# Cross attention over 32 batches: half-tile score banks, a third maximum bank, a new order of projections, and the maximum split on the vector engine

## The reference, cut to what matters

```python
x = _layernorm(x + self_attention(x))            # one head, causal mask
x = _layernorm(x + cross_attention(x, ctx_1024)) # 16 heads of 8, relative bias
x = _layernorm(x + ffn(x))                       # 128 -> 512 -> 512 -> 512 -> 128, gated

# cross attention, for each of the 32 batches
q = shape(query_states @ wq, T); k = shape(key_value_states @ wk, S); v = shape(key_value_states @ wv, S)
scores = jnp.einsum('bhtd,bhsd->bhts', q, k) + bias        # T = 56, S = 1500
weights = jax.nn.softmax(scores, axis=-1)
attn = jnp.einsum('bhts,bhsd->bhtd', weights, v)
return attn.transpose(...).reshape(B, T, D) @ wo
```

## Time and profile before

| | |
|---|---|
| median of 3 runs | 1085.17 us (1084.59 to 1091.04) |
| the profiled execution | 1093.1 us, its span 1091.3 us |
| PE busy | 969.3 us, 89% of the span |
| DVE busy | 721.8 us, 66% |
| ACT busy | 605.5 us, 55% |
| POOL busy | 421.6 us, 39% |
| mean granted TensorE clock | 0.952 of 2.4 GHz |

### The profile page before, as it was taken

The page is one execution under the profiler, slowest core; times in us unless marked ns, Lnnn a source line. Parts: engine busy times, 40 slices in busy tenths (PEclk is TensorE's granted clock), DMA queues, the critical chain, the costliest instruction groups (busy, mean ns, idle before and its releaser), DMA issues. The chain is left out here.

```text
span 1091.3 us, 25611 instructions
## 1 busy us (share of the span) xinstructions
PE 969.3 (89%) x10410; PEld 657.2 (60%) x10410; DVE 721.8 (66%) x1510; ACT 605.5 (55%) x1071; POOL 421.6 (39%) x418
## 2 busy tenths in 40 slices
PE   6754579999999999999999999989999988799996
PEld 3542256666666666666666666666666666545564
DVE  6565447878778877878778878876777774540014
ACT  2321157666667666666666666666666656352232
POOL 7330535554444555554444555554444400000000
PEclk9866689999999999999999999998999999899999
DMA  7507665555666655555665755554665420300000
GB/s 228 192 10 163 117 190 178 164 177 178 191 177 204 185 176 179 163 178 178 191 194 161 209 179 177 164 179 147 188 181 162 137 78 2 109 1 1 1 9 25
DMA packets 57388, 156.10 MB, mean 143 GB/s; under 512 B 23936, under 2 KB 36152, under 8 KB 54200
## 3 DMA queue, kind: packets, MB, share of 16 engines
q1 hardware_dynamic: 56744, 152.85, 48.1%
q10 hardware_dynamic: 528, 1.63, 0.4%
HBM read 111.63 MB, written 42.63 MB: 141 GB/s over the span
## 5 line engine op out<-in xcount | busy, mean ns | idle before, releaser
L769 ACT ACTIVATE e_sb<-st_ps 128x896 f32<-128x896 f32 (+1 forms) x384 | 354.1, 925 | 153.0 <-DVE st_ps L714 93.5
L108 DVE TENSOR_REDUCE cmax<-max_ps 112x1 f32<-112x512 f32 x512 | 337.6, 683 | 150.5 <-PE max_ps L98 150.4
L98 PE MATMUL max_ps<-kst,qst 111*112 111x512 bf16 x760 | 283.8, 401 | 37.8 <-PEq L117 14.1
L611 PEld LDWEIGHTS st_ps<-qst,kst 114*128 114x128 bf16 (+1 forms) x3072 | 191.7, 101 | 88.7 <-issue 41.8
L821 POOL TENSOR_TENSOR kpart<-k_left,kpart 128x500 bf16<-128x500 f32 x90 | 102.7, 1141 | 352.4 <-ACT k_left L787 347.8
L611 PE MATMUL st_ps<-qst,kst 114*128 114x112 bf16 (+1 forms) x3072 | 215.7, 213 | 19.5 <-DMA qst<-nmp 18.3
L105 DVE CUSTOM_DVE_ANT_0 near_out<-max_ps,near_nat 112x476 bf16<-112x476 f32 x248 | 154.0, 649 | 26.4 <-PE max_ps L98 26.4
L98 PEld LDWEIGHTS max_ps<-kst,qst 111*112 111x112 bf16 x760 | 92.2, 130 | 106.8 <-DVE cmax L108 38.9
L641 PE MATMUL pv_ps<-e_sb,vals 128*32 128x168 f32 (+1 forms) x3072 | 150.0, 313 | 0.3 <-ACT e_sb L769 0.3
L685 PEld LDWEIGHTS misc<-wv,ctxt 128*128 128x128 f32 (+1 forms) x768 | 99.6, 193 | 15.8 <-ACT vals L754 11.8
L641 PEld LDWEIGHTS pv_ps<-e_sb,vals 128*32 128x32 f32 (+1 forms) x3072 | 80.4, 109 | 47.1 <-issue 34.6
(11 more groups left out here) (127 smaller groups left out, 941.1 us busy)
## 6 DMA issues: line engine op xcount, KB each, us to landing
kst<-kparts SPq DMA_DIRECT2D x192, 375.0 KB, 6.2
kparts<-kpart SPq DMA_DIRECT2D x90, 375.0 KB, 2.7
ctxt<-in_ctxT SPq DMA_DIRECT2D x32, 750.0 KB, 7.4
qst<-qslots SPq DMA_DIRECT2D x192, 28.0 KB, 6.4
qslots<-qst SPq DMA_DIRECT2D x4, 672.0 KB, 11.2
kparts<-kst SPq DMA_DIRECT2D x6, 375.0 KB, 3.1
h<-in_h SPq DMA_DIRECT2D x2, 1024.0 KB, 8.6
qst<-nmp SPq DMA_DIRECT2D x96, 1.8 KB
```

Of the source, the lines that this page charges most:

```text
L98: return nc.tensor.matmul(dst[0:TT, 0:hi - lo], m.qst[0:M_ROW, r, p, :], m.kst[0:M_ROW, r, p, lo:hi], start=True, stop=True)
L108: return nc.vector.tensor_reduce(m.cmax[:, r, c, p:p + 1], src[0:TT, 0:BOUND[c + 1] - BOUND[c]], AX.X, ALU.max)
L611: mm = nc.tensor.matmul(st_ps[0:K, j % 2, p // 4, (p % 4) * TT:(p % 4 + 1) * TT], m.kst[0:AUG, u % RING, p, j * P:j * P + K], m.qst[0:AUG, ...
L769: nc.scalar.activation(e_sb[0:K, j % E_RING, :].rearrange("p (a c) -> p a c", a=2), st_ps[0:K, j % 2, :, 0:HALF], ACT.Exp).then_inc(s_ex, 1)
```

## The change

- `st_ps` becomes three single banks. A tile's scores are made in two halves of 4 pairs, half h of tile j being number w = 2 x (12 b + j) + h, in bank w mod 3; each half is signalled, waited for and exponentiated by itself (448 columns). PE waits before a half until exponential w - 3 is done. The near additions are made by halves too.
- `max_ps` and `near_out` have three buffers; a chunk waits for the reduction three before it.
- `misc` in the steps 0 to 6: v, k, v, k, v, k, den (was v, v, v, den, k, k, k). In the iteration ahead of batch 0 the keys are at steps 1, 3, 5. The reciprocals are made in steps 6 and 7 (were 4 and 5), x_own and its sums in step 10 (was 9).
- The negated maximum is split into three bfloat16 parts by DVE before it is transposed, by four operations on 112 x 8, each waiting for the one before. PE transposes the 24 columns with a bfloat16 identity, ACT makes one copy (two before), and one DMA (three before) brings the three rows to `qst`. POOL's split of the maximum is gone, and POOL makes all three key splits before the multiplication by `own`.
- On ACT the copy of `pv_ps` in step 1 comes after the copies for `misc`.

The core of the diff:

```diff
 E_RING = 4
...
         PAIRED = ST // 2
-        HEAD_MISC = {4: ("k", 0, 3), 5: ("k", 1, 3), 6: ("k", 2, 3), M0: ("nmt", 0, 1),
+        HEAD_MISC = {1: ("k", 0, 3), 3: ("k", 1, 3), 5: ("k", 2, 3), M0: ("nmt", 0, 1),
                      9: ("v", 0, 1), 10: ("v", 1, 1), 11: ("v", 2, 1)}
-        MISC = {0: ("v", 0, 1), 1: ("v", 1, 1), 2: ("v", 2, 1), 3: ("den", 0, -1),
-                4: ("k", 0, 3), 5: ("k", 1, 3), 6: ("k", 2, 3), M0: ("nmt", 0, 1)}
-        NM, REC_A, REC_B, XH = M0 - 1, 4, 5, 9
+        MISC = {0: ("v", 0, 1), 1: ("k", 0, 3), 2: ("v", 1, 1), 3: ("k", 1, 3), 4: ("v", 2, 1), 5: ("k", 2, 3),
+                6: ("den", 0, -1), M0: ("nmt", 0, 1)}
+        NM, REC_A, REC_B, XH = M0 - 1, 6, 7, 10
...
                 if j == 0:
-                    pe.wait_ge(s_md[u % 2], filled(g, u, 2, 48))
-                wait(pe, s_ex, batch(g, u) * ST + j - 1)
+                    pe.wait_ge(s_md[u % 2], filled(g, u, 2, 16))
                 K = st_rows(j)
-                for p in range(PAIRS):
-                    mm = nc.tensor.matmul(st_ps[0:K, j % 2, p // 4, (p % 4) * TT:(p % 4 + 1) * TT],
-                                          m.kst[0:AUG, u % RING, p, j * P:j * P + K],
-                                          m.qst[0:AUG, u % RING, p, :],
-                                          start=True, stop=True)
-                mm.then_inc(s_st, 1)
+                for h in range(2):
+                    w = 2 * (batch(g, u) * ST + j) + h
+                    wait(pe, s_ex, w - ST_BANKS + 1)
+                    for p in range(4):
+                        mm = nc.tensor.matmul(st_ps[0:K, w % ST_BANKS, p * TT:(p + 1) * TT],
+                                              m.kst[0:AUG, u % RING, 4 * h + p, j * P:j * P + K],
+                                              m.qst[0:AUG, u % RING, 4 * h + p, :],
+                                              start=True, stop=True)
+                    mm.then_inc(s_st, 1)
 
             def max_chunk(g, u, item):
 
...
+                wait(pe, s_mr, batch(g, u + lag) * CHUNKS + n - MAX_BANKS + 1)
+                max_scores(nc, m, max_ps[:, n % MAX_BANKS, :], r, c, p).then_inc(s_mx, 1)
 
             def value_pair(g, u, t):
 
                 n = batch(g, u)
-                wait(pe, s_ex, n * ST + t + 2)
+                wait(pe, s_ex, 2 * (n * ST + t + 2))
                 if t == 0:
                     wait(pe, s_xr, n)
                     wait(pe, s_ve, 3 * n + 3)
...
                         pe.wait_ge(s_nm, n + 1)
-                        nc.tensor.transpose(misc[0:PAIRS, 0:TT], nmax[:, :], m.ident[0:TT, 0:TT]).then_inc(s_nt, 1)
+                        pe.wait_ge(s_ib, 1)
+                        nc.tensor.matmul(misc[0:3 * PAIRS, 0:TT], nm3[:, :, :].rearrange("q i p -> q (i p)"),
+                                         ident_b[:, :], start=True, stop=True).then_inc(s_nt, 1)
 
...
-                        dve.wait_ge(s_st, b * ST + j + 1)
-                        if j == 0:
-                            t, near = st_ps[:, 0, :, 0:HALF], m.near_t0[:, :].rearrange("p (a c) -> p a c", a=2)
-                        else:
-                            t = st_ps[0:NEAR - P, 1, :, 0:HALF].rearrange("p a (h t) -> p a h t", t=T)
-                            t = t[:, :, :, T - NEAR + P:T]
-                            near = m.near_t1[:, :].rearrange("p (a h t) -> p a h t", a=2, t=T)
-                            near = near[:, :, :, T - NEAR + P:T]
-                        nc.vector.tensor_tensor(t, t, near, ALU.add).then_inc(s_nb, 1)
+                        for h in range(2):
+                            w = 2 * (b * ST + j) + h
+                            dve.wait_ge(s_st, w + 1)
+                            if j == 0:
+                                t, near = st_ps[:, w % ST_BANKS, 0:HALF], m.near_t0[:, h * HALF:(h + 1) * HALF]
+                            else:
+                                t = st_ps[0:NEAR - P, w % ST_BANKS, 0:HALF].rearrange("p (h t) -> p h t", t=T)
+                                t = t[:, :, T - NEAR + P:T]
+                                near = m.near_t1[:, h * HALF:(h + 1) * HALF].rearrange("p (h t) -> p h t", t=T)
+                                near = near[:, :, T - NEAR + P:T]
+                            nc.vector.tensor_tensor(t, t, near, ALU.add).then_inc(s_nb, 1)
                     if j == XH and live(g, u - 1):
                         dve.wait_ge(s_ro, b)
                         nc.vector.tensor_tensor(x_own[:, :], x_sb[:, :], rec[:, :], ALU.mult).then_inc(s_xo, 1)
                     for lag, n, c, p in max_items(g, u, j):
                         dve.wait_ge(s_mx, (b + lag) * CHUNKS + n + 1)
-                        reduce_scores(nc, m, max_ps[:, n % 2, :], (u + lag) % 2, c, p).then_inc(s_mr, 1)
+                        reduce_scores(nc, m, max_ps[:, n % MAX_BANKS, :], (u + lag) % 2, c, p).then_inc(s_mr, 1)
                     if j == NM and live(g, u + 1):
                         dve.wait_ge(s_mr, (b + 2) * CHUNKS)
                         wait(dve, s_nt, b + 1)
+                        wait(dve, s_nm, b + 1)
                         nc.vector.tensor_reduce(nmax[:, :], m.cmax[:, (u + 1) % 2, :, :].rearrange("q c p -> q p c"),
-                                                AX.X, ALU.max, negate=True).then_inc(s_nm, 1)
+                                                AX.X, ALU.max, negate=True).then_inc(s_n0, 1)
+                        dve.wait_ge(s_n0, b + 2)
+                        nc.vector.tensor_copy(nm3[:, 0, :], nmax[:, :]).then_inc(s_n1, 1)
+                        dve.wait_ge(s_n1, 2 * b + 3)
+                        nc.vector.tensor_tensor(nm_left[:, :], nmax[:, :], nm3[:, 0, :], ALU.subtract).then_inc(s_n1, 1)
+                        dve.wait_ge(s_n1, 2 * b + 4)
+                        nc.vector.tensor_copy(nm3[:, 1, :], nm_left[:, :]).then_inc(s_n2, 1)
+                        dve.wait_ge(s_n2, b + 2)
+                        nc.vector.tensor_tensor(nm3[:, 2, :], nm_left[:, :], nm3[:, 1, :], ALU.subtract).then_inc(s_nm, 1)
                     if live(g, u - 1):
                         if j == REC_A:
                             dve.wait_ge(s_dr, b)
...
                     if live(g, u):
-                        w = b * ST + j
-                        if j < 2:
-                            act.wait_ge(s_nb, 2 * b + j + 1)
-                        act.wait_ge(s_st, w + 1)
+                        K = st_rows(j)
                         wait(act, s_pv, b * PAIRED + j // 2 - 1)
-                        K = st_rows(j)
-                        nc.scalar.activation(e_sb[0:K, j % E_RING, :].rearrange("p (a c) -> p a c", a=2),
-                                             st_ps[0:K, j % 2, :, 0:HALF], ACT.Exp).then_inc(s_ex, 1)
-                    if j == 1 and live(g, u - 1):
-                        act.wait_ge(s_pv, b * PAIRED)
-                        wait(act, s_xo, b - 1)
-                        nc.scalar.copy(x_sb[:, :], pv_ps[:, 0:PIECES * T]).then_inc(s_xr, 1)
+                        for h in range(2):
+                            w = 2 * (b * ST + j) + h
+                            if j < 2:
+                                act.wait_ge(s_nb, 4 * b + 2 * j + h + 1)
+                            act.wait_ge(s_st, w + 1)
+                            nc.scalar.activation(e_sb[0:K, j % E_RING, h * HALF:(h + 1) * HALF],
+                                                 st_ps[0:K, w % ST_BANKS, 0:HALF], ACT.Exp).then_inc(s_ex, 1)
                     user = misc_user(g, u, j)
...
                             if live(g, u):
-                                act.wait_ge(s_md[u % 2], filled(g, u, 2, 48))
-                            nc.scalar.copy(nmp[:, 0, :], misc[0:PAIRS, 0:TT])
-                            nc.scalar.copy(nm_left[:, :], misc[0:PAIRS, 0:TT]).then_inc(s_nr, 1)
+                                act.wait_ge(s_md[u % 2], filled(g, u, 2, 16))
+                            nc.scalar.copy(nmp[:, :], misc[0:3 * PAIRS, 0:TT]).then_inc(s_nr, 1)
+                    if j == 1 and live(g, u - 1):
+                        act.wait_ge(s_pv, b * PAIRED)
+                        wait(act, s_xo, b - 1)
+                        nc.scalar.copy(x_sb[:, :], pv_ps[:, 0:PIECES * T]).then_inc(s_xr, 1)
 
             run(iteration)(act)
...
+            nc.gpsimd.tensor_copy(ident_b[:, :], m.ident[0:TT, 0:TT]).then_inc(s_ib, 1)
...
                 b = batch(g, u)
                 split_k(g, u, 0)
+                split_k(g, u, 1)
...
                     pool.wait_ge(s_ro, b)
-                split_k(g, u, 1)
-                if live(g, u + 1):
-                    done = 3 * (b + 1)
-                    pool.wait_ge(s_nr, b + 2)
-                    nc.gpsimd.tensor_tensor(nmp[:, 1, :], nm_left[:, :], nmp[:, 0, :],
-                                            ALU.subtract).then_inc(s_np, 1)
-                    pool.wait_ge(s_np, done + 1)
```

(14 more changed lines are left out.)

20 lines of the change are left out of this document (10 added, 10 removed).

## The result

The changed kernel takes 1122.91 us, median of four runs (1121.5 to 1125.14); the kernel before took 1087.73 on the same chips. The ratio is 1.0325, 95% interval 1.0281 to 1.0369: 3.3% slower. The profiled execution took 1121.78 us with a span of 1120.0.

The account below looks back on a forecast made before the run. PE with its waits was taken as the bound; the changed loop, 14.71 + 11.03 = 25.75 us against 24.5, gave +1.25 a batch, +35 over 28 batches, less about 4: 1085.2 + 31 = 1116 us, range 1078 to 1140.

Parts of the forecast that it names:

- The loop: Second half of S1 to den's copy on PE and ACT, then DVE back to S1: 25.75 us a batch against 24.5.
- first part: PE and ACT from the second half of S1 (second tile's scores) to the end of den's copy: 14.71 us.
- one ahead of nmt: PE's wait before the maximum's transpose, for DVE's split: 1.23 us, or 1.5 with DVE's lateness by the reciprocal.
- The key wait: PE after each key projection, waiting for ACT's copies: 0.48 us each, three replacing one, +0.96 us of PE per batch.
- the chain: Four dependent DVE operations on 8 columns that split the maximum: 4 x 0.20 = 0.80 us.
- the 4 us that the forecast took off for the end: 1.9 us for a wait at 912.23 and about 2 for the batches without key projections.
- This decides: Reciprocals (1.11 and 0.84 us) and maximum split on DVE now stand just ahead of the dense steps 8 to 11.
- PE with these pieces is the bound: Kernel before: 21.9 us of PE work a period plus some 2.6 us of standing still in pieces.
- nobody waits for that room: POOL's key splits start earlier, giving POOL and SP's stores of key parts room that was said to be unneeded.
- 1 (DVE never behind): Rival, chance 0.17: only misc order and maximum split cost, 24.6 us a period, about 1084 us, up to 1096.
- 2 (little comes back): Rival, chance 0.15: waits go, nmt's wait is 0.43 to 0.91, period 23.8 to 24.3 us, 1061 to 1075 us.
- 3: Rival, chance 0.10: waits cost more than their length, by score-half hand-overs or a lower granted clock, 1130 to 1152 us.

Follow-up runs that it names:

- after_nmt9: The changed kernel with nmt at step 9 instead of step 8: 1120.9 us, ratio 1.0288.
- best_4_2: `old_direct` with the third key projection at step 7, nmt at step 9, four half-tile score banks and two maximum banks: 1069.73 us, ratio 0.9832.
- no_recip: The changed kernel with both reciprocals cut to one column: 1110.58 us, ratio 1.0207.
- banks_alone: The kernel before with only the three half-tile score banks and three maximum banks: 1084.08 us, ratio 0.9962.
- old_direct: The kernel before with the change's banks, one DMA for the maximum rows and a one-part bfloat16 maximum written by the reduction: 1051.23 us, ratio 0.9645.
- no_split: `old_order` with POOL's three operations per key part cut from 500 columns to one: 1073.41 us, ratio 0.9869.
- one_part_direct: The changed kernel, new order kept, with a one-part bfloat16 maximum written by the reduction instead of the four-operation split: 1093.56 us, ratio 1.0036.
- old_order: The changed kernel with the old order of projections and reciprocals, and the old order on ACT and POOL: 1171.19 us, ratio 1.0772.

## Why the prediction was right, and where it was not

Forecast was a regular period of 25.75 us, from a loop; measured 25.74. Forecast were 1116 us, measured 1122.91.

*The loop, right in its course; that it fits to 0.01 is luck.* The forecast's first part runs from the second half of S1 (535.89) to the end of den's copy (550.53 + 0.39): 15.03 us, 14.71 forecast. From there to the next second half (561.63) are 10.71, 11.03 forecast. Each part missed by 0.32, and the two misses cancel. The waits were where they were said to be: three behind the keys, one ahead of nmt (1.39 in the prediction's way of counting, forecast 1.23, or 1.5 with DVE's lateness), one for a maximum bank in step 0 (0.18, forecast 0.5), one of 0.23 by its row and 0.39 from start to start at the second half of S1. An exponential of 448 columns takes 0.554, and the near additions 1.16 for two. `after_nmt9` supports the loop: it took away the largest of PE's waits and the period did not move.

*The key wait, mis-sized by 0.10.* From a key projection to the next S are 0.84 and then 2.30 (538.42 to 540.72) with 0.83 + 0.89 of work in them, so a wait costs 0.58, not 0.48: a projection that starts behind one takes 0.10 longer. The earlier trace rows show that already, 0.94 from 553.50 to the next S against 0.84 from 551.35. Two of these waits lie in the first part of the sum (0.20), and the copies and exponentials behind the third key add 0.08. What made up for them lies on DVE: the chain's links are 0.205 apart as forecast, but the second reciprocal starts 0.70 after the first of them and not 0.80 (554.24, inside the last one), and from it to the near addition are 6.08 and not 6.24. (The prediction's own parts of its 1.31, 0.20 + 0.47 + 0.58, are 1.25.)

*The 7 us between 1116 and 1123.* A fourth run of the kernel before took 1090.29 and moved its median from 1085.17 to 1087.73: 2.6 of the 7. The rest is the difference of the medians, 35.2 where 31 was forecast. The two traces divide theirs (28.7) by the near additions. The 28 periods from the second batch on add 26.1: 28 x 1.23 = 34.4, less 8.3 us by which some batches of the kernel before are longer than 24.51. The first period adds 2.4 and the last two take off 4.1. The stretch behind the last near addition adds 3.9, the one ahead of the first 0.4. So the 4 us that the forecast took off for the end were right, and it left out the first batch and the end of the block. Of the 3.9, 2.8 lie behind the last copy of `pv_ps`, where no edit was made; in the thirteen traces this last stretch takes between 162.2 and 168.3 us. (The forecast's average of 24.72 took the last start of the earlier trace rows, 913.8, for that of an addition like the first; it is the small one of tile 1.)

*The longer batches, not explained in the forecast.* The 8.3 us are six of the 28 periods of the kernel before, 24.73 to 27.16 long. The longest, 27.16, ends with this wait (timeline of the kernel before):

```profile
737.45 0.93 PE L611 MATMUL st_ps<-qst,kst 114*128 114x112 bf16 x8 [2.52 <-DMA qst<-nmp]
```

The maximum rows came late, PE stood still, and the granted clock from 737.40 to 741.00 was 0.50. At 815.06 PE waited 1.64 for them. The two kernels with three DMAs for the rows wait for them in nearly every batch; the eleven with one DMA show a single such wait behind the first batch (0.67, at the end of `best_4_2`), and the changed kernel's 31 periods are 27 of 25.74 and four shorter ones. The forecast put this transfer at 0.24 to 0.5 a batch and 1.9 once. Whether the median run of the kernel before has fewer long batches no trace shows.

*"This decides", wrong.* The reciprocals at steps 6 and 7 lay in the loop, as worked out, and yet they decided next to nothing (`no_recip`, 0.25 us). A second loop, without them, was only 0.25 shorter. The sum was right because the longer one was found; the reason given for it was not the one that a remedy could have used.

*What bounds the kernel before, incomplete.* "PE with these pieces is the bound" overlooked that the maximum rows' way through POOL and three DMAs was as long. The wait of 0.24 at 563.33 was counted as a small piece that goes away. It was the visible end of a loop that takes back most of a gain elsewhere: the banks bring 0.27 with it (`banks_alone`) and 24.35 - 23.33 = 1.02 without it.

*The balance, by runs.* From 24.51: banks and direct rows -1.18 (`old_direct`), the chain +0.82 (`no_split`, `one_part_direct`), the new order +1.59 (`one_part_direct` against `old_direct`). Together 24.51 - 1.18 + 0.82 + 1.59 = 25.74; these are steps from run to run, so they must add up, and only the chain's term was measured twice. Of the order's 1.59, two more key waits at 0.58 are 1.16 if they add, and the second halves of S1 and the reciprocals are candidates for the rest, which no run divides.

*What the prediction did not see at all* is what the new order is good for. It said of POOL's earlier splits that nobody waits for that room. With the split on DVE, it is all-important: at the old places the chain meets POOL's key splits and costs 3.98 (27.31 - 23.33), at the new places POOL is done just in time (its last split of the period runs from 552.20 to 553.33, the first cast starts at 553.54) and it costs 0.82. So the order costs 1.59 us where the chain is absent and gains 1.57 where it is present.

*The rivals.* 1 (DVE never behind) fell with DVE's timeline. 2 (little comes back) fell at the chain, 0.82 where it needed under 0.5, but its other half was true and larger than it said: without chain and order, the freed waits give 1.18. 3: in a regular batch the clock was granted in full after the 1.26 us (1.00 from 554.40 to 558.00). It did fall after 2.78 us of standing still in `old_order`, and in the last batch of the changed kernel after a wait of 1.73, so the mechanism exists here, at a longer wait.

## What to carry to other kernels

Look for all loops that are nearly as long as the bounding one before summing up gains: here two edits worth 0.16 and 0.27 us a batch alone were worth 1.18 together, and a remedy for the named bottleneck gave 0.25. When small operations are moved to the vector engine, see what GpSimd runs at that time, and give them a place where it is idle. And ask first whether they are needed: leaving the split out was better than both places tried for it.

## What the hardware showed unexpectedly

- A DVE operation on 112 x 8 takes 168 ns (subtraction of two SBUF operands) or 171 ns (cast) and, in the time of a POOL operation on 128 x 500, 1006 and 1057 ns on average: it ends just after POOL's. In `old_order` a reduction of 24 to 8 columns (0.18 at 550.03, POOL busy to 550.22) and the near maxima, whose input is partly in PSUM (0.65 at 552.66, POOL busy), are not held up. It goes the other way too: POOL's split at 553.82 in `old_order` lasts 1.42 where others last 1.13, with the x_own product of DVE (two SBUF operands) at 553.81 beside it.
- After 2.78 us in which PE stood still, the granted clock in `old_order` was 0.50 from 552.80 to 556.00 (1.2 of 2.4 GHz) and 0.98 behind that, in every batch; the mean fell from 0.952 to 0.909. A wait of 1.26 us in the changed kernel's regular batches left it at 1.00. Between these the length of the wait doesn't decide alone: after 1.73 us (nmt at 932.22 in the changed kernel) it was 1.00 to 933.70 and 0.53 from there to 937.10, after 1.89 us (912.23 in the kernel before) it stayed at 1.00.
- A float32 projection that starts behind a wait takes 0.10 us longer up to the next S than one in the stream: 0.94 against 0.84 for keys, and 1.00 against 0.89 for values in the changed kernel (539.72 to 540.72).
